# Value products of two probability tiles issued together in every second slot of an attention kernel

## What is computed

```python
g = group_norm(x)                              # 32 groups of 6 channels
q, k, v = qkv_w @ g                            # 6 heads of 32 channels each
attn = softmax(q^T k * 32**-0.5)               # per head 1024 x 1024
out = x + proj_w @ (attn v) + proj_b
```

## Time and profile before

| | us |
|---|---|
| median of 3 runs | 1725.47 (1725.34 to 1728.06) |
| the profiled execution's own time | 1727.79 |
| its span, first to last instruction | 1725.9 |
| PE busy | 1609.9 (93% of the span) |
| POOL busy | 1323.5 (77%) |
| ACT busy | 1231.0 (71%) |
| DVE busy | 1192.1 (69%) |

### The profile page before, as it was taken

The page is one execution under the profiler, slowest core; times in us unless marked ns, Lnnn a source line. Parts: engine busy times, 40 slices in busy tenths (PEclk is TensorE's granted clock), DMA queues, the critical chain, the costliest instruction groups (busy, mean ns, idle before and its releaser), DMA issues.

```text
span 1725.9 us, 29564 instructions
## 1 busy us (share of the span) xinstructions
PE 1609.9 (93%) x9056; PEld 537.0 (31%) x9056; DVE 1192.1 (69%) x2086; ACT 1231.0 (71%) x2001; POOL 1323.5 (77%) x645
## 2 busy tenths in 40 slices
PE   2689999998999999999999999999999999999982
PEld 1233233332333333333333323332333333233220
DVE  2487778776777767776787767777677777777710
ACT  1238796876869677785978768696777869677770
POOL 3128798886879778886988868797788879788891
PEclk9989999999999999998999999999999999999995
DMA  1404151321514123251513315151232514140202
GB/s 56 96 1 83 36 92 33 85 54 52 105 50 93 41 60 71 55 101 52 88 28 87 59 52 105 50 93 40 60 72 55 101 50 73 51 76 18 58 25 75
DMA packets 74283, 109.26 MB, mean 63 GB/s; under 512 B 26176, under 2 KB 39040, under 8 KB 74112
## 3 DMA queue, kind: packets, MB, share of 16 engines
q1 hardware_dynamic: 74112, 107.13, 29.0%
HBM read 42.99 MB, written 12.98 MB: 32 GB/s over the span
## 4 chain that ended last, share of the span: by engine, by line
PE 80%; ACT 8%; issue 3%; DMA 1%; DVE 1%; SPq 0%; POOL 0%; ACTq 0%; POOLq 0%; DVEq 0%
PE heads_ps L552 21%; PE max_ps L462 19%; PE scores_ps L537 19%; PE sums_ps L569 7%; ACT probs L692 5%; PE extra_ps L520 2%; PE extra_ps L524 2%; PE extra_ps L521 2%; PE extra_ps L522 2%; PE extra_ps L525 2%; PE extra_ps L484 1%; ACT xhat_b L644 1%; PE extra_ps L483 1%; ACT x_res L622 1%; DMA inv_sb<-inv_rows 1%
## 5 line engine op out<-in xcount | busy, mean ns | idle before, releaser
L833 DVE TENSOR_REDUCE half_max<-max_ps 128x1 f32<-128x512 f32 x1536 | 1009.3, 685 | 381.1 <-PE max_ps L462 365.8
L692 ACT ACTIVATE probs<-scores_ps,exp_scale 128x512 f32<-128x512 f32 x1536 | 992.3, 689 | 365.2 <-PE scores_ps L537 360.9
L753 POOL TENSOR_TENSOR prob_pairs<-probs 128x1024 f32<-128x1024 f32 x384 | 898.6, 2362 | 259.0 <-ACT probs L692 258.2
L537 PE MATMUL scores_ps<-q_stack,k_stack 98*128 98x512 f16 x1536 | 590.2, 385 | 27.4 <-ACT probs L692 11.1
L462 PE MATMUL max_ps<-k_stack,q_stack 96*128 96x512 f16 x1536 | 597.6, 391 | 7.2 <-DVE half_max L833 4.8
L552 PE MATMUL heads_ps<-probs,v_sb 128*32 128x512 f32 x3072 | 416.3, 614 | 0.1
L462 PEld LDWEIGHTS max_ps<-k_stack,q_stack 96*128 96x128 f16 x1536 | 150.2, 98 | 544.1 <-issue 438.2
L759 POOL TENSOR_TENSOR prob_pairs<-prob_pairs 128x1024 f32<-128x1024 f32 x96 | 224.2, 2359 | 0.0
L537 PEld LDWEIGHTS scores_ps<-q_stack,k_stack 98*128 98x128 f16 x1536 | 150.1, 98 | 227.7 <-ACT probs L692 149.1
L569 PE MATMUL sums_ps<-prob_pairs,ones 128*32 128x512 f32 x1152 | 154.3, 608 | 3.2 <-POOL prob_pairs L753 3.2
L552 PEld LDWEIGHTS heads_ps<-probs,v_sb 128*32 128x32 f32 x3072 | 60.7, 108 | 133.9 <-issue 128.5
(11 more groups left out here) (93 smaller groups left out, 1046.3 us busy)
## 6 DMA issues: line engine op xcount, KB each, us to landing
q_stack<-qk_hi SPq DMA_DIRECT2D x96, 128.0 KB, 4.4
k_stack<-qk_hi SPq DMA_DIRECT2D x96, 128.0 KB, 5.3
inv_sb<-inv_rows SPq DMA_DIRECT2D x48, 256.0 KB
x_res<-x SPq DMA_DIRECT2D x16, 768.0 KB, 5.9
out<-x_res SPq DMA_DIRECT2D x16, 768.0 KB, 4.6
x_sb<-x SPq DMA_DIRECT2D x16, 512.0 KB, 6.4
x_sb<-x SPq DMA_DIRECT2D x32, 256.0 KB, 7.6
q_stack<-qk_lo SPq DMA_DIRECT2D x48, 128.0 KB, 4.0
```

The costliest lines, as they stand in the source:

```text
L537: pe.matmul(scores_ps[:, u_bank(s, u), :], k_stack[0:SHIFTED, st.parity, h, P * tile:P * (tile + 1)], q_stack[0:SHIFTED, st.parity, h, HAL ...
L692: nc.scalar.activation(probs[:, a, s % RING, HALF * half:HALF * (half + 1)], scores_ps[:, u_bank(s, u), :], ACT.Exp, scale=exp_scale[:, 0: ...
L753: nc.gpsimd.tensor_tensor(prob_pairs[:, a, q, :], probs[:, a, (s - 1) % RING, :], probs[:, a, s % RING, :], ALU.add).then_inc(pairs_added, 1)
L833: nc.vector.tensor_reduce(half_max[:, a, tile, half:half + 1], max_ps[:, bank, :], AX_X, ALU.max).then_inc(max_read[bank], 1)
```

## The change

```diff
@@ -580,11 +580,12 @@
                     for u in range(SCORE_UNITS):
                         if st.attend:
                             score(st, s, u)
-                        if u == 1:
-                            if s == 0 and st.tail:
-                                weigh(st.b - 1, 1 - st.parity, SLOTS - 1)
-                            elif s > 0 and st.attend:
-                                weigh(st.b, st.parity, s - 1)
+                        if u == 1 and s % PAIR == 0:
+                            for tile in range(s - PAIR, s):
+                                if s == 0 and st.tail:
+                                    weigh(st.b - 1, 1 - st.parity, SLOTS + tile)
+                                elif s > 0 and st.attend:
+                                    weigh(st.b, st.parity, tile)
                         if u >= 2 and st.extra(s) is not None:
                             fill(st, s, u - 2)
                         if u == COUNT_UNIT:
```

## The result

| | before | after |
|---|---|---|
| median, us | 1726.76 (4 runs) | 1788.03 (4 runs, 1786.44 to 1791.56) |
| span of the profiled execution, us | 1725.9 | 1784.6 |
| PE, ACT, DVE, POOL busy, us | 1610, 1231, 1192, 1324 | 1605, 1222, 1187, 1323 |
| one batch in the middle, us | 97.37 | 101.56 |

The changed kernel is slower by 61 us: the ratio is 1.0353, with a 95% interval of 1.0332 to 1.0374. 1784 us were forecast, in a range of 1764 to 1812.

The account below looks back on a forecast made before the run. PE was taken as the bound, with ACT's slack limited by two score banks. Per batch, 6.7 us waits added less 2.8 gained is 3.9; 16 batches give 62, less 4, so 58 on 1725.5: 1784 us, range 1764 to 1812.

Parts of the forecast that it names:

- What bounds PE: PE sets the time, busy 96.77 of 97.40 us in a batch; two score banks keep ACT's 20 us slack from helping.
- rule 1: PE's times: score plus row maximum 0.44 us; a float32 group adds 1.09, projection extras 0.65 and 0.43, v extras 0.41.
- What the change removes: Second value group directly behind the first costs 0.85 instead of 1.09 us: 0.24 us per pair, 2.8 us a batch.
- The rule of bare weight loads: Skill page: loads overlap matmuls in flight only where row groups differ, so nearly all of the 0.24 us would stay.
- its rival at 1828 us: Second value group costs as much as one alone; waits grow 6.7 us a batch, nothing gained: 103 us more; chance 10%.
- What it adds: Six to eight scores without a float32 group between: PE's waits per batch rise from 2.7 to 9.4 us, 6.7 added.
- the pace of 0.44 against 0.60 us: In score runs without a float32 group, PE offers scores every 0.44 us while ACT takes them every 0.60 us.
- DVE at 0.4 us: With DVE at no cost, a batch grows 3.5 instead of 3.9 us; its three banks are nearly never last.
- a wait of PE for DVE: Named sign that the prediction is wrong, alongside PE waiting for POOL or for the clock.
- The term of 4 us: In five batches after loop jumps, near half clock, new waits fall away, 0.6 to 0.8 us each: -4 us.
- The clock rival: PE's idle time lowers the clock; one twentieth of the time at 1.2 GHz costs 80 us: 1865 us; chance 4%.
- The faster rival: Edges saved without growing waits: 1680 us; decided by fewer than 2.8 us of new waits a batch; chance 4%.

Follow-up runs that it names:

- the halved kernel: Changed kernel with every exponential and row-maximum reduction over 256 of 512 columns, ACT's copies left long: 1692.5 us, a batch of 96.44 us.
- the last two kernels: Changed kernel with nine pairs joined and count group in unit 1: 1714.4 us; with five pairs joined and count groups placed slot by slot by the rules: 1703.5 us.

## Why the prediction was right

- **What bounds PE.** Right. For seven pairs of slots (from slots 6, 8, 10, 14, 16, 18 and 22) rule 1 prices all of the work, with 0.85 us for the second group. Added to the waits that the prediction lists, this gives each of them to 0.15 us. The largest misses are slots 16 and 17 (9.46 us worked out, 9.60 measured) and 18 and 19 (9.16 and 9.24); slots 22 and 23 are 8.08 and 8.07.
- **What the change removes.** Right: 0.24 us per pair was worked out, 0.23 is measured by parting the groups again. The second group costs 0.86 us, at the low end of its bounds. The rule of bare weight loads does not hold here: its rival at 1828 us is refuted by the loads in the trace and by the 0.86 us.
- **What it adds.** Right in kind, a little small in size: 4.19 us of growth in a batch with 2.8 us gained make 7.0 us of new waits; 6.7 were worked out. Of those the exponentials with the reductions are the larger share, since halving both takes the change's cost in a batch from 4.2 to 1.0 us, but not the only one. ACT's copies between exponentials are worth 1.3 to 1.4 us of a batch even when all exponentials are short. The prediction counted them in its rules, but its text put the pace of 0.44 against 0.60 us first and named copies and activations in two pairs of slots only. The expectation of the halved kernel, which left them out, missed by some 45 us.
- **DVE at 0.4 us.** A little undersized: 0.6 us in a batch. The prediction named a wait of PE for DVE as a sign of being wrong. By its letter the sign came: PE's loads of the row maxima wait for DVE three times in a batch, 1.2 us in all, where before they did not. At this size it leaves the account as it is.
- **The sum.** 58 us were added, 61 measured, and here errors partly cancel. A batch at the full clock grew by 4.2 us and not by 3.9, which is 5 us more in 16 batches. The term of 4 us for the batches after the loop's five jumps back was too small: in the traces they grow by 0.5, 0.9, 1.0, 4.6 and 2.4 us, 9.5 in all, where 5 x 4.2 would be 21. So 11 us are given back and not 4. The reason given, that new waits fall away at the low clock, is not what shows. In the fourth of these batches the mean granted clock is nearly the same in both kernels (0.966 before, 0.968 after), and it grows by 4.6 us, no less than a batch at the full clock. In the first three it is 0.983 to 0.985 instead of 0.950 to 0.967: PE spends less time at the low level. Why the low level ends sooner in the changed kernel isn't shown. Against this the first batch of all grows by 5.8 us; its granted clock is 0.951 after and 1.000 before. These clocks are of one trace of each kernel, and over a whole run the changed kernel's lie between 0.974 and 0.977.
- **The clock rival** is refuted: the granted clock is 1.00 in the batch, with PE idle for 4.7 us of it instead of 0.6.
- **The faster rival** was decided by its own mark: 7.0 us of new waits in a batch, where under 2.8 would have been needed. That the two effects can be had apart, the last two kernels show.

## What to carry to other kernels

When one engine hands work to another through two banks, the other's average slack is of use to it only as far as the time between two hand-overs allows. Long work that does not need the banks is the cover under which the other engine catches up. Where it stands counts as much as how long it is: spread it, and join pieces only where an extra or another long group still parts the hand-overs. To judge such a move, take four distances from the trace (the first engine's work per hand-over, the delay until the second one starts, its pace, and the time until the bank is free), replay them over one period of the kernel, and test them on the kernel as it is before using them on the change.

## What the runs showed of the hardware

- A float32 group of four matmuls on four column quarters costs 1.09 us alone and 0.86 us directly behind another. Of the difference 0.09 us stand ahead of it (0.31 us from the score's start to the group's, instead of 0.22) and 0.14 us up to the next matmul's start (1.00 instead of 0.86). A fp16 row-maximum matmul between two groups brings the edges back, 0.23 us per pair.
- Weight loads for a column quarter ran beside a matmul in flight on the same rows and columns, one load ahead, also from one group into the next: twelve loads had started when eight matmuls had.
- The pace of a 128x512 exponential in a run, 0.59 to 0.61 us, is shorter than the 0.69 us that a single one shows; the time to the release of its bank was 0.74 us after its start.
- After the last jump back of the loop the joined group took 3.64 us, nearly twice the 1.92 us that it takes ten us later: this is the low level of the clock, 1.2 GHz. The page's row of the clock has a 9 there as elsewhere, since each of its slices averages 45 us.

```profile
1248.21 3.64 PE L552 MATMUL heads_ps<-probs,v_sb 128*32 128x512 f32 x16
1258.87 1.92 PE L552 MATMUL heads_ps<-probs,v_sb 128*32 128x512 f32 x16
```
